# Wider register loads with masked counts, and single steps in place of pairs in the edge attention of a graph kernel

## The reference

```python
h = jnp.maximum(_layernorm(x), 0.0)
# attention layer
h = (h @ W.T).reshape(n, 8, 32)
alpha = einsum('ehd,hd->eh', h[src], a_src) + einsum('ehd,hd->eh', h[dst], a_dst)
enc = relu(edge_attr @ edge_W.T + edge_b).reshape(-1, 8, 32)
alpha = alpha + sum(enc * h[dst], axis=-1)
alpha = where(alpha >= 0, alpha, 0.2 * alpha)
ex = exp(alpha - segment_max(alpha, dst)[dst])
attn = ex / maximum(segment_sum(ex, dst)[dst], 1e-10)
x = x + segment_sum(h[src] * attn[..., None], dst).reshape(n, 256) + bias
# two convolutions (256 -> 128 -> 64), each
#   out = segment_sum((h @ W)[s] * norm[:, None], d) + b, batch norm, relu
# and a last product over the three concatenated feature sets
```

## Time and profile before

| | |
|---|---|
| median of three runs | 8406.8 us (8395.62 to 8412.13) |
| the profiled execution | 8473.6 us, its span 8471.7 us |
| mean granted TensorE clock | 0.696 |
| busy over the span: PE, DVE, ACT, POOL | 4795.9, 3617.7, 2112.1, 4758.0 us |
| attention stage, 110 slots | 340 to 3559 us |
| first and second convolution | 3744 to 5998 us, 6097 to 8385 us |
| the rest (tables, node product, between the stages, end) | 711 us |

### The profile page before, as it was taken

One profiled execution on the slowest core, in us unless ns is written; L12 is line 12 of the kernel. 1 busy time (PEld: TensorE's weight loads), 2 busy tenths in 40 slices (PEclk: granted clock), 3 DMA queues, 4 the chain that ended last, 5 costly groups with the idle time before them and its releaser, 6 DMA issues. The chain is left out here.

```text
span 8471.7 us, 115634 instructions
## 1 busy us (share of the span) xinstructions
PE 4795.9 (57%) x27189; PEld 3615.4 (43%) x27410; DVE 3617.7 (43%) x10996; ACT 2112.1 (25%) x6088; POOL 4758.0 (56%) x4797
## 2 busy tenths in 40 slices
PE   3677877777777777753333333333544544445444
PEld 3455545455545555543333333333434444444443
DVE  6566655556656556652222222222322222222224
ACT  4455555555555555540000000000100000000001
POOL 3644444444444444356666666666366666666665
PEclk9788888888988888875555555555655555555555
DMA  6645545445555455451111111111211111111114
GB/s 205 196 147 150 146 146 147 142 144 148 148 146 150 143 148 148 120 170 44 46 46 45 45 46 46 46 45 46 50 28 29 29 29 29 29 29 29 29 25 134
DMA packets 519666, 776.49 MB, mean 92 GB/s; under 512 B 145864, under 2 KB 396512, under 8 KB 519021
## 3 DMA queue, kind: packets, MB, share of 16 engines
q0 software_dynamic: 176288, 376.45, 17.6%
q1 hardware_dynamic: 305126, 359.86, 13.5%
q10 hardware_dynamic: 37783, 34.96, 1.3%
HBM read 693.70 MB, written 81.14 MB: 91 GB/s over the span
## 5 line engine op out<-in xcount | busy, mean ns | idle before, releaser
L1722 POOL DMA_INDIRECT c_g<-conv_table,c_idx x3128 | 2973.1, 950 | 1684.0 <-issue 890.9
L1801 PE MATMUL c_sums<-c_g,acc 128*128 x7040 | 1646.6, 405 | 2431.0 <-issue 1617.1
L1801 PEld LDWEIGHTS c_sums<-c_g,acc 128*128 128x128 f32 x7040 | 1526.7, 308 | 2654.5 <-issue 2603.0
L1029 POOL DMA_INDIRECT acc<-gat_table,ga_idx x1564 | 1526.0, 976 | 1725.9 <-DVE ga_wg L1282 1189.8
L1765 DVE TENSOR_TENSOR acc<-acc,c_sums 128x128 f32 (+1 forms) x1760 | 443.7, 252 | 3292.3 <-DMA ga_h<-h_parts 1228.7
L1410 PE MATMUL ga_sums<-ga_wg,ga_S 128*128 128x265 f32 x3520 | 1061.6, 442 | 148.0 <-issue 107.5
L1360 PE MATMUL ga_dstp<-ga_oht,ga_h 128*128 128x256 bf16 x5280 | 892.2, 305 | 369.2 <-issue 332.6
L1215 DVE SCALAR_TENSOR_TENSOR ga_prod<-acc,ga_a_dst,ga_dstp 128x512 f32<-128x512 f32 x880 | 632.4, 741 | 748.1 <-issue 463.7
L1410 PEld LDWEIGHTS ga_sums<-ga_wg,ga_S 128*128 128x128 f32 x3520 | 701.0, 212 | 398.7 <-issue 200.2
L1360 PEld LDWEIGHTS ga_dstp<-ga_oht,ga_h 128*128 128x128 bf16 x5280 | 561.3, 108 | 616.9 <-issue 436.2
L1750 DVE TENSOR_SCALAR acc<-iota_row,c_dcol 128x128 f32<-128x128 f32 x3520 | 806.5, 308 | 0.2 <-issue 0.2
(11 more groups left out here) (249 smaller groups left out, 3623.6 us busy)
## 6 DMA issues: line engine op xcount, KB each, us to landing
ga_h<-h_parts SPq DMA_DIRECT2D x880, 192.0 KB
ga_dl<-dl_rows SPq DMA_DIRECT2D x110, 512.0 KB
c_g<-conv_table,c_idx POOLq DMA_INDIRECT x3128
acc<-gat_table,ga_idx POOLq DMA_INDIRECT x1564
h_parts<-h_split SPq DMA_DIRECT2D x14, 1344.0 KB
gat_table<-h_out SPq DMA_DIRECT2D x14, 952.0 KB
x_rows<-md_x SPq DMA_DIRECT2D x14, 896.0 KB
fc_x<-x_rows ACTq DMA_DIRECT2D x98, 128.0 KB
```

The costliest lines, as they stand in the source:

```text
L1029: pool.indirect_dma_start(G[:, (v * PC + j) * HROW:(v * PC + j + 1) * HROW], None, gat_table, bass.IndirectOffsetOnAxis(idx[:, c:c + 1], 0 ...
L1722: pool.indirect_dma_start(G[:, c % (2 * SLOTS), :], None, table, bass.IndirectOffsetOnAxis(idx[:, c:c + 1], 0)).then_inc(rows_in[c // 2 % ...
L1801: last = nc.tensor.matmul(sums[:, b % R, 0:width], S[:, u * CH + 2 * b + j, :], flat[:, bass.ds(slots[b] * (2 * width) + j * width, width) ...
```

## The change

It has two parts. First, register loads: where two loads of eight stood one behind the other, one load of sixteen takes both rows of a table (`both_rows`). The counts are loaded as whole four-byte words in place of their lower halves, and each wait masks the register with `COUNTS` (the lower 15 bits). `need_tab` and its DMA fall away, since `row_tab` now holds both rows. This touches ScalarE and VectorE in the attention stage and TensorE and SyncE in the convolutions; GpSimd's load keeps its form. Second, the slot of the attention stage: TensorE and VectorE go through the eight steps singly. A sum of unit k-1, then quantum k+2, and after every second quantum the dots of two steps; on VectorE a product, a flush and a weighing in each step, with the small operations spread over steps 0, 1, 2, 4 and 5. ScalarE's order stays.

```diff
@@ -778,7 +778,8 @@
     QD = 4
-    LISTS = 8
+    COUNTS = (1 << 15) - 1
+    LISTS = 7
     with ExitStack() as ctx:
@@ -810,8 +811,7 @@
         dcol = [sb(ctx, f"ga_dcol{u}", [P, CH]) for u in range(2)]
-        row_tab = [sb(ctx, f"ga_row_tab{u}", [1, UL], I32) for u in range(2)]
-        need_tab = [sb(ctx, f"ga_need_tab{u}", [1, UL], U16) for u in range(2)]
+        row_tab = [sb(ctx, f"ga_row_tab{u}", [1, 2, UL], I32) for u in range(2)]
         sum_tab = [sb(ctx, f"ga_sum_tab{u}", [1, 2, UL], I32) for u in range(2)]
@@ -894,6 +894,15 @@
 
+        def both_rows(tab, eng, first, second):
+
+            why = "unit numbers are clamped where they are worked out"
+            _, regs = nc.values_load_multi_w_load_instructions(
+                tab[0:1, :, :].rearrange("o k n -> o (k n)"), engines=[eng], min_val=0, max_val=max(first, second),
+                skip_runtime_bounds_check_because=why)
+            return ([nc.s_assert_within(r, 0, first, skip_runtime_bounds_check_because=why) for r in regs[0:UL]],
+                    [nc.s_assert_within(r, 0, second, skip_runtime_bounds_check_because=why) for r in regs[UL:2 * UL]])
+
         with nc.Block() as block:
@@ -946,9 +955,7 @@
                     sp.dma_start(lflags[u][:, :], AP(line_rows.tensor, m * LINE, [[0, HEADS], [1, LINE]])).then_inc(list_in[u], 16)
-                    sp.dma_start(row_tab[u][:, :], AP(unit_table.tensor, m * UL + UNITS, [[0, 1], [1, UL]])).then_inc(list_in[u], 16)
-                    with nc.allow_non_contiguous_dma(reason="eight counts"):
-                        sp.dma_start(need_tab[u][:, :], low_halves(AP(unit_table.tensor, m * UL + 2 * UNITS, [[0, 1], [1, UL]]))).then_inc(list_in[u], 16)
+                    sp.dma_start(row_tab[u][0:1, :, :], AP(unit_table.tensor, m * UL + UNITS, [[0, 1], [UNITS, 2], [1, UL]])).then_inc(list_in[u], 16)
 
@@ -1073,13 +1080,12 @@
                     take_waits(act, held)
-                    return (registers(row_tab[u][:, :], mybir.EngineType.Activation, 0, NS - 1),
-                            registers(need_tab[u][:, :], mybir.EngineType.Activation, READY + 1, READY + 1 + UNITS // PB))
+                    return both_rows(row_tab[u], mybir.EngineType.Activation, NS - 1, READY + 1 + UNITS // PB)
 
...
                     slot_of, need = regs
-                    act.wait_ge(rows_ready, need[b])
+                    act.wait_ge(rows_ready, need[b] & COUNTS)
                     rows = G[:, bass.ds(slot_of[b] * PROWS, PROWS)].rearrange("p (j c) -> p j c", c=HROW)[:, :, S0:HROW]
@@ -1300,43 +1306,37 @@
                         take_waits(dve, held)
-                        tiles = registers(sum_tab[w][0:1, 0, :], mybir.EngineType.DVE, 0, TILES - 1)
+                        tiles, slot_of = both_rows(sum_tab[w], mybir.EngineType.DVE, TILES - 1, NS - 1)
                         last_tiles.append(tiles[UL - 2:UL])
-                        slot_of = registers(sum_tab[w][0:1, 1, :], mybir.EngineType.DVE, 0, NS - 1)
-                    for k in range(0, QS, 2):
-                        for q in (k, k + 1):
-                            if a:
-                                product(n + q, q)
-                        for q in (k, k + 1):
-                            if a and t * QS + q < TILES // GT:
-                                nc.vector.memset(acc[:, (t * QS + q) * GT:(t * QS + q + 1) * GT, :], 0.0).then_inc(s_zero, 1)
+                    for k in range(QS):
+                        if a:
+                            product(n + k, k)
+                        if tail and k < 2:
+                            flush(x.at(-3), UL - 2 + k, late[k])
+                        if a and t * QS + k < TILES // GT:
+                            nc.vector.memset(acc[:, (t * QS + k) * GT:(t * QS + k + 1) * GT, :], 0.0).then_inc(s_zero, 1)
                         if c and k == 2:
...
                             rescale(o, tiles[0])
-                        for q in (k, k + 1):
-                            if tail and k == 0:
-                                flush(x.at(-3), UL - 2 + q, late[q])
-                            if c and k:
-                                flush(o, q - 2, tiles[q - 2])
+                        if c and k >= 2:
+                            flush(o, k - 2, tiles[k - 2])
                         if b and k == 0:
...
                             scan_on(x)
-                        for q in (k, k + 1):
-                            if c:
-                                weigh(o, w, q, slot_of[q])
-                        if b and k == 0:
+                        if b and k == 1:
                             scan_back(x)
                             last_and_first(m)
+                        if c:
+                            weigh(o, w, k, slot_of[k])
                         if b and k == 2:
...
                             carried(m, v)
+                        if b and k == 5:
+                            tops(m)
                         if more and k >= 4:
                             transposed(t + 1, k - 4)
-                            transposed(t + 1, k - 3)
-                        if b and k == 4:
-                            tops(m)
 
@@ -1413,27 +1413,25 @@
                     t, m, v = x.at(), x.at(-1), x.odd(-1)
-                    for k in range(0, QS, 2):
-                        for n in (k - 2, k - 1):
-                            if k == 0 and tail:
-                                add(x.at(-3), UL + n)
-                            if k and c:
-                                add(x.at(-2), n)
+                    for k in range(QS):
+                        if k == 0 and tail:
+                            add(x.at(-3), UL - 1)
+                        if k and c:
+                            add(x.at(-2), k - 1)
                         if b and k == 2:
...
                             carries(m, v)
+                        if a and k < QS - 2:
+                            quantum(t, k + 2)
+                        if more and k >= QS - 2:
+                            quantum(t + 1, k + 2 - QS)
+                        if a and k % 2:
+                            dot(t, k - 1)
+                            dot(t, k)
                         if b and k == 6:
...
                             turn_back(m)
-                        for q in (k + 2, k + 3):
-                            if a and q < QS:
-                                quantum(t, q)
-                            if more and q >= QS:
-                                quantum(t + 1, q - QS)
-                        if a:
-                            dot(t, k)
-                            dot(t, k + 1)
                     if a:
@@ -1632,7 +1630,7 @@
     _, regs = nc.values_load_multi_w_load_instructions(
-        low_halves(row), engines=[eng], min_val=USED, max_val=USED + UNITS,
+        row if eng == mybir.EngineType.SP else low_halves(row), engines=[eng], min_val=USED, max_val=USED + UNITS,
         skip_runtime_bounds_check_because="unit numbers are clamped where they are worked out")
@@ -1647,12 +1645,13 @@
     SLOTS = NB * PB
+    COUNTS = (1 << 15) - 1
     with ExitStack() as ctx:
...
         table_row = sb(ctx, f"{name}_table", [1, 3, UNITS], I32)
-        utile_row, slot_row, need_row = (table_row[0:1, k, :] for k in range(3))
+        utile_row = table_row[0:1, 0, :]
         free_f = sb(ctx, f"{name}_free_f", [1, BLOCKS])
@@ -1686,7 +1685,7 @@
 
-                    sp.wait_ge(sum_done, used)
+                    sp.wait_ge(sum_done, used & COUNTS)
                     sp.sem_inc(ring_free, 1)
@@ -1786,15 +1785,15 @@
                 def iteration(m, u, i, fc, more):
-                    _, slots = nc.values_load_multi_w_load_instructions(
-                        slot_row[0:1, bass.ds(m * UL, UL)], engines=[mybir.EngineType.PE], min_val=0, max_val=NB * PB - 1,
-                        skip_runtime_bounds_check_because="pair numbers are taken modulo the slots where they are worked out")
-                    _, needs = nc.values_load_multi_w_load_instructions(
-                        low_halves(need_row[0:1, bass.ds(m * UL, UL)]), engines=[mybir.EngineType.PE], min_val=READY + 1, max_val=READY + 1 + UNITS,
-                        skip_runtime_bounds_check_because="pair numbers are clamped where they are worked out")
+                    why = "pair numbers are clamped, and taken modulo the slots, where they are worked out"
+                    _, regs = nc.values_load_multi_w_load_instructions(
+                        table_row[0:1, 1:3, bass.ds(m * UL, UL)], engines=[mybir.EngineType.PE], min_val=0, max_val=READY + 1 + UNITS,
+                        skip_runtime_bounds_check_because=why)
+                    slots = [nc.s_assert_within(r, 0, NB * PB - 1, skip_runtime_bounds_check_because=why) for r in regs[0:UL]]
+                    needs = regs[UL:2 * UL]
                     for b in range(UL):
                         n = m * UL + b
-                        pe.wait_ge(rows_ready, needs[b])
```

(1 more changed line is left out.)

## The result

The changed kernel takes 8550.9 us (8539.68 to 8569.08, four runs), the kernel before 8409.5 on the same chip (8395.62 to 8417.55, four runs): ratio 1.0162, 95% interval 1.0145 to 1.0179. It is slower by 141 us where the prediction had it faster by 83; time, sign and range of the prediction were wrong. The profiled executions stand nearer to each other (spans 8567.2 and 8471.7 us, 95.5 apart), since the profiled one before is 64 us above its median and the one after 18, so what follows accounts for those 95.5 us and not for all 141.

What follows compares the result with a forecast made beforehand. TensorE's pace was taken to bound the attention stage, GpSimd's gathers the convolutions. Loads -70, order +22, stretches -15 and convolutions -20 sum to -83 us, ratio 0.9902; on the 8,406.8 us median 8,324 us, range 8,190 to 8,450.

Steps and rivals of the forecast that it cites:

- What bounds the kernel: TensorE paces the attention stage, 22.7 us busy of 29.3 a slot; GpSimd's gathers set the convolutions' floor, 3,910 us.
- slow stretches: Attention stage, TensorE's small matmuls far apart while GpSimd gathers: single steps space gather blocks, -15 us, bounds -125 and +40.
- Part 2: Attention stage, TensorE and VectorE in single steps: 0.8 us a slot new waits against 0.7 old, +11; ScalarE another +11 us.
- ScalarE's load: Attention stage, ahead of the fourth one-hot: one load of sixteen takes 0.8 us instead of 2.27, gaining 70 us.
- SyncE's DMA: Attention stage: one list DMA fewer a slot brings node loads and attributes 0.7 us earlier; not late, so no gain.
- The convolutions: Shorter TensorE register loads let gather runs reach further before waiting for SyncE's release: 20 us gained, bounds 0 and 147.
- A: Rival, attention stage: the stretches give the gain back, as TensorE slows earlier; 8,390 to 8,423 us, chance 0.12.
- Rival B: Attention stage: the one-step hand-over fails, TensorE waits at quanta 5 to 8 and sums; about 8,510 us, chance 0.17.
- C: Rival, attention stage and convolutions: stretches come from gathers in lumps; -346 us, about 8,065, with half 8,235; chance 0.14.
- D: Rival, register loads: a load of sixteen costs as two, each register having its price whatever the form; 8,414 us, chance 0.05.

Runs made afterwards that it cites:

- after_ahead: Changed kernel, but VectorE makes the products of steps 3 and 5 at the end of steps 2 and 4; 8505.8 us, ratio 1.0088.

## Why the prediction was wrong, step by step

**What bounds the kernel.** TensorE's pace and the slow stretches were read rightly, but as time in which only TensorE's own matmuls are slow. That VectorE gets TensorE's signals late was told of the convolutions, from the earlier trace rows, and not carried over to the attention stage.

**The failed step** is the sentence of Part 2 that lets weighing k end "1.3 us behind" the sum it needs, and with it the stepping through a slot that finds 0.8 us of new waits. Both take a signal as there when its matmul ends. On a late chip the line product's is 3.6 us late at the median. In pairs VectorE waited for late signals at its products and flushes, and had made both products of the pair before it turned to the small operations (one wait at the line scan, 1.2 us). In singles the waits stand at the small operations, and the next product stands right behind them. The term was +11 (+22 with ScalarE's), the net of 0.8 us of new waits a slot and 0.7 of old ones gone, and measured, as idle time at the three places, 601 us in place of 35. Against that other places lost some 430 (627 to 199), since long gaps replace the many small ones, so that TensorE's idle time rose by 137 us in all and the stage by 131. That the hand-over costs nothing where signals are prompt is shown by the prompt chips: with the loads of the change, singles and pairs stand at 0.9815 and 0.9808 to 0.9810.

**ScalarE's load** was put at 0.8 us and took 1.02: near the upper bound of two loads, 1.2. Per register that is 64 ns. The Trainium skill, "Runtime: NRT & Kernel Launch", section Instruction fetch mechanics, has about 200 ns a register; measured here it is a third of that, for sixteen as for eight. By the same page of the Trainium skill, section The ~15µs preamble/postamble breakdown, that instruction loads registers from HBM, which the prediction left out; these loads read rows in SBUF, so the two figures are not of the same thing. The gain at the fourth one-hot came (57.0 to 2.4 us of TensorE's gaps; forecast 70 in time). On prompt chips the loads alone won 132 to 136 us. What they are worth on a late chip was not run alone, so I can't split the 141 us there into a gain and a loss.

**SyncE's DMA "not late now, so nothing"** was wrong on prompt chips with the old loads (53 us), and right with the wide one.

**The convolutions**, forecast -20: -31 in the profile of the first chip, with the 28 us of release waits as the cause I had named. The kernel before has only one trace on a late chip, so how far this difference scatters is not known. On prompt chips there is nothing to win, because no such wait exists.

**The slow stretches**, forecast -15: blocks did come apart (270 waits for 222; runs of exactly eight gathers, with pauses of up to 1 us inside, 92 for 117), but the price of a run rose, from 3.8 to 5.1 us of TensorE's gaps in a run of eight and in the 3 us behind it, so that those runs cost 467 us in place of 440. A, that the stretches give the gain back, is nearer to this than the forecast. So the sign of this step was wrong.

**Rival B** named the side, two of the places (the later quanta and the sums) and nearly the size (8,510). Its reason, that TensorE's 2.3 and VectorE's 2.2 us a step are nearly equal, is not what happened: on prompt chips they are just as equal and nothing is lost. That its time came within 41 us is luck. C did not occur on the first chip, and D's price "whatever the form" is refuted by the 1.02 us; within the four-byte form sixteen do cost nearly what two loads of eight did (547 ns each on ScalarE).

## What to carry to other kernels

Look in the trace at how long a consumer starts after the matmul it needs, not only at who waits: where signals come late, the work that an in-order engine has already handed over is what counts, and a finer order gives it away. Put what another engine will ask for next ahead of the small operations that wait for that engine's own results, and then ask which instruction is now the one behind them. In `after_ahead` this won back part of the loss on a late chip; on a prompt one it was not tried. And time a change on more than one chip before its sign is believed: here the loads alone are as fast as the full change on prompt chips (6,808 and 6,819 us against 6,819), and on late ones the full change loses; how the loads alone do there was not run.

## What the runs showed of the hardware

The same kernel takes 8,410 to 8,430 us on some chips and 6,944 to 6,951 on others. Single instructions last as long on both: a gather in the convolutions 0.947 us at the median, a matmul of the weighted sums 387 ns at the upper clock level. The difference lies where GpSimd gathers: there TensorE's signals arrive late on the one kind, by 8.5 us in the wait shown, and on the other within 0.02 us in all 110 cases counted; and in the attention stage TensorE's clock is at its lower level for 874 us on the one and 24 on the other. A register load costs 64 to 75 ns a register in words of four bytes, for eight as for sixteen (0.55 to 0.60 and 1.02 to 1.13 us), and three times that for every second halfword.
